# Summing x and beta of the last batch ahead in DRAM, earlier gathers and earlier weight loads in a fused attention and mixture-of-experts kernel

## The reference, cut to what matters

```
u   = ln_c(x)                                    # over the width, eps 1e-6
o   = conv1x1(channel_attention(u), wo)          # 8 heads of 16 channels, softmax over channels
x1  = x + (o - mean_w(o)) * rsqrt(var_w(o) + 1e-5) * gamma + beta       # over the width
t   = tokens(x1)                                 # 16 x 16384 x 128: rows of 128 numbers
z   = ln_t(t)
logits = z @ gate_w.T + gate_b ;  probs = softmax over the tokens of a batch
vals, idx = top 8 tokens of each of 64 experts, in each batch
pooled    = sum over the 8 of vals * z[idx]      # one row for each batch and expert
y   = gelu([pooled,1] @ weight1[e]) ; out_e = [y,1] @ weight2[e]
result = t ; result[idx] += vals * out_e
```

## Time and profile before

| | us |
|---|---|
| median of 3 runs (lowest, highest) | 2142.67 (2136.2, 2142.91) |
| the profiled execution | 2155.56 |
| its span, first to last instruction | 2153.8 |

### The profile page before, as it was taken

One profiled execution on the slowest core, in us unless ns is written; L12 is line 12 of the kernel. 1 busy time (PEld: TensorE's weight loads), 2 busy tenths in 40 slices (PEclk: granted clock), 3 DMA queues, 4 the chain that ended last, 5 costly groups with the idle time before them and its releaser, 6 DMA issues.

```text
span 2153.8 us, 42420 instructions
## 1 busy us (share of the span) xinstructions
PE 1873.0 (87%) x11917; PEld 1286.6 (60%) x11917; DVE 1822.8 (85%) x4612; ACT 1882.0 (87%) x5020; POOL 1939.2 (90%) x2068
## 2 busy tenths in 40 slices
PE   6999999999999999999999999999999987636991
PEld 6866666666666666666666666666666643213570
DVE  4689999999999898989899999999999899624670
ACT  6899999999999999999999999999999987743420
POOL 5799999999999999999999999999999999961387
PEclk9999999999999999999999999999999998765995
DMA  5498888887888888888788888888788676694963
GB/s 188 157 262 222 228 223 206 226 229 216 218 218 235 224 227 210 224 231 222 215 216 231 229 224 220 212 229 227 213 222 223 178 182 162 165 263 124 282 104 32
DMA packets 111068, 447.92 MB, mean 208 GB/s; under 512 B 10575, under 2 KB 52404, under 8 KB 61684
## 3 DMA queue, kind: packets, MB, share of 16 engines
q1 hardware_dynamic: 81140, 302.61, 42.9%
q0 software_dynamic: 29696, 142.61, 34.2%
HBM read 306.78 MB, written 138.41 MB: 207 GB/s over the span
## 4 chain that ended last, share of the span: by engine, by line
ACT 38%; POOL 21%; issue 17%; PE 16%; DVE 5%; ACTq 1%; DMA 1%; POOLq 0%; SPq 0%; DVEq 0%
ACT U L553 16%; POOL U L430 8%; POOL U L435 7%; ACT zT L516 6%; ACT UT L510 6%; PE G L747 4%; ACT LTS L580 3%; ACT LTS L525 3%; PE T L729 3%; PE O L680 2%; POOL zn L451 2%; POOL out_dram L490 2%; PE T L736 1%; ACT zn L574 1%; POOL U L442 1%
## 5 line engine op out<-in xcount | busy, mean ns | idle before, releaser
L553 ACT ACTIVATE U<-xa,nA,rA 128x128 f32<-128x128 f32 x1948 | 803.7, 483 | 2.1 <-issue 1.3
L747 PEld LDWEIGHTS G<-UT 128*128 128x128 f32 x4096 | 536.8, 192 | 226.5 <-issue 225.3
L430 POOL TENSOR_TENSOR U<-U,bet 128x512 f32<-128x512 f32 x512 | 651.4, 1272 | 2.2
L435 POOL TENSOR_TENSOR U<-U,rO 128x512 f32<-128x512 f32 x512 | 532.2, 1040 | 20.3 <-ACT rO L533 19.3
L747 PE MATMUL G<-UT 128*128 128x128 f32 x4096 | 542.0, 275 | 0.0
L680 PE MATMUL O<-U,MT 128*128 128x512 f32 x1024 | 529.5, 599 | 3.0 <-DVE U L938 3.0
L451 POOL TENSOR_TENSOR zn<-U,rZ 128x512 f32<-128x512 f32 x414 | 446.6, 1079 | 11.0 <-ACT rZ L564 10.3
L936 DVE BATCH_NORM_STATS2 stO<-O 128x6 f32<-128x256 f32 x1024 | 386.8, 423 | 50.2 <-PE O L680 49.5
L729 PE MATMUL T<-ident,U 128*128 128x128 f32 x2048 | 324.3, 281 | 119.1 <-ACT UT L510 108.6
L729 PEld LDWEIGHTS T<-ident,U 128*128 128x128 f32 x2048 | 224.6, 142 | 318.1 <-issue 314.1
L954 DVE BATCH_NORM_STATS2 stA<-xa 128x6 f32<-128x256 f32 x1024 | 386.8, 426 | 31.8 <-DMA xa<-in_x 28.5
(11 more groups left out here) (151 smaller groups left out, 1655.0 us busy)
## 6 DMA issues: line engine op xcount, KB each, us to landing
xa<-in_x SPq DMA_DIRECT2D x128, 1024.0 KB, 6.3
U<-in_x POOLq DMA_DIRECT2D x128, 1024.0 KB, 10.8
out_dram<-U SPq DMA_DIRECT2D x128, 1024.0 KB, 8.6
U<-in_L_ffn_weight SPq DMA_DIRECT2D x112, 256.0 KB
LTS<-in_L_ffn_weight SPq DMA_DIRECT2D x16, 256.0 KB
xa<-out_dram,UT POOLq DMA_INDIRECT x64
out_dram<-U,UT POOLq DMA_INDIRECT x64
zT<-in_L_ffn_weight SPq DMA_DIRECT2D x1, 128.0 KB
```

What stands on the lines that cost most here:

```text
L430: gp.tensor_tensor(rows(a, i), rows(a, i), bet_b, ALU.add).then_inc(S["gb"], 1)
L435: gp.tensor_tensor(rows(a, i), rows(a, i), rO[:, i // 2 % 2, i % 2 * TI:(i % 2 + 1) * TI].unsqueeze(2).to_broadcast([P, TI, W]), ALU.mult) ...
L553: last = sc.activation(utile(a, i, j), xa[:, k % XR, h * W:(h + 1) * W], ACT.Identity, scale=rA[:, k % 2, h:h + 1], bias=nA[:, k % 2, h:h ...
L747: last = te.matmul(G[:, 0:P], v, v, start=(i == 0 and j == 0), stop=(i == NI - 1 and j == TI - 1))
```

## The change

Three things are changed.

1. For the last batch (chunks 120 to 127, `X_BETA` = 120) POOL no longer adds beta. Instead x + beta is made ahead in DRAM, in the place of the result where the last batch will be stored. In step 100 SP writes beta, repeated over 16 image rows, from SBUF into the first 1 MB piece; in steps 116, 132, ..., 212 it copies that piece to the other seven. From step 260 on, one in 16 steps, POOL issues eight DMAs that add a piece of x (DRAM) to a piece of the result (DRAM). The accumulates of the last batch then read from there instead of from x.
2. `S_GATH` is 540, the gathers of 13 batches (52) stand three to two steps, and the first part of `PARTS` is at step 536 with 13 batches. The 12 other gathers stand behind the loop: four each for batches 13, 14 and 15. `Z_ALL` follows `S_GATH`, from 473 to 464, which moves items 467 and 471 of `zn` from POOL to ACT.
3. The weights of experts 0 to 15 stand in SP's body, one expert in two steps from step 540 on, each waiting only for the part of batch 14 that it overwrites. Experts 16 to 19 wait for items 0 to 7 of the last batch and the stores of its first two chunks, instead of the whole.

```diff
-PARTS = ((545, 0, 14), (576, 14, 15))
-S_GATH = 549
+PARTS = ((536, 0, 13), (577, 13, 15))
+S_GATH = 540
...
+X_BETA = 15 * NK
+S_PRE, S_SUM = 100, 260
...
         def _(sp): body
+                    if (m := ahead(b, t, S_PRE)) is not None:
+                        if m == 0:
+                            sp.dma_start(place(out_v, 0).rearrange("c b (h w) -> c (b h) w", w=W),
+                                         bet[:, :].unsqueeze(1).to_broadcast([P, TC, W])).then_inc(s_pre, 16)
+                        else:
+                            sp.wait_ge(s_pre, 16)
+                            sp.dma_start(place(out_v, m), place(out_v, 0)).then_inc(s_pre, 16)
...
+                    e, r = divmod(b[0] * NI + t - S_GATH, 2)
+                    if r == 0 and 0 <= e < EQN:
+                        wait_zn(sp, (NB - 2, None), e * 2 + 1)
+                        sp.wait_ge(s_store[e // 2], 16 * (NB // 2))
+                        weights(e)
...
-            wait_zn(sp, (NB - 2, None), NI - 1)
-            for k in range(NK):
-                sp.wait_ge(s_store[k], 16 * (NB // 2))
-            for e in range(EQN):
-                weights(e)
-            wait_zn(sp, (NB - 1, None), NI - 1)
-            for k in range(NK):
+            wait_zn(sp, (NB - 1, None), 2 * IC - 1)
+            for k in range(2):
                 sp.wait_ge(s_store[NK + k], 16 * (NB // 2))
...
         def _(pool): body
+                    if (m := ahead(b, t, S_SUM)) is not None:
+                        pool.wait_ge(s_pre, 16 * NX)
+                        gp.dma_start(place(out_v, m), place(x_v, m), accum_op=ALU.add).then_inc(s_sum, 16)
-                    if r := item(b, t, L_BETA):
+                    if (r := item(b, t, L_BETA)) and r[0][0] * NI + r[1] < X_BETA * IC:
...
-                                     x_v[:, bass.ds(bv, 1), k * CW:(k + 1) * CW],
+                                     (x_v if n < X_BETA else out_v)[:, bass.ds(bv, 1), k * CW:(k + 1) * CW],
...
-                    if 0 <= g < Q * (NB - 2):
+                    for g in range(max(0, 3 * g // 2), min(3 * (g + 1) // 2, Q * (NB - 3))):
```

More of the change, by code:

```diff
@@ L202, in program @@
         s_store = [sem(f"s_store{i}") for i in range(2 * NK)]
-        s_setup_dve = sem("s_setup_dve")
+        s_setup_dve = sem("s_setup_dve"); s_pre = sem("s_pre"); s_sum = sem("s_sum")
         names = ("a_bn a_ln a_rstd a_nmu u_ready tru ut_ready gram g_copied a1 a1s att att_s "
@@ L276, in wait_zn, with place, ahead @@
             wait(eng, S["zn_act"], by_act[n])
+        def place(v, m):
+            b, k = divmod(X_BETA + m, NK)
+            return v[:, b:b + 1, k * CW:(k + 1) * CW]
+        NX = NB * NK - X_BETA
+        def ahead(b, t, start):
+            m, r = divmod(b[0] * NI + t - start, 16)
+            return m if r == 0 and 0 <= m < NX else None
         def bodies(eng, body):
@@ L326, in body @@
                                      U[:, a[0] % 2, k:k + 1, :]).then_inc(s_store[n], 16)
-            bodies(sp, body)
+                    e, r = divmod(b[0] * NI + t - S_GATH, 2)
[3 more added lines that the diff above has]
+                        weights(e)
             def weights(e):
@@ L337, in weights @@
                              w2v[:, e:e + 1, :, :]).then_inc(landed, 16)
-            wait_zn(sp, (NB - 2, None), NI - 1)
-            for k in range(NK):
-                sp.wait_ge(s_store[k], 16 * (NB // 2))
-            for e in range(EQN):
-                weights(e)
-            wait_zn(sp, (NB - 1, None), NI - 1)
-            for k in range(NK):
+            bodies(sp, body)
+            wait_zn(sp, (NB - 1, None), 2 * IC - 1)
+            for k in range(2):
                 sp.wait_ge(s_store[NK + k], 16 * (NB // 2))
@@ L439, in body @@
                         a, k = r
-                        pool.wait_ge(S["gb"], cnt(a, NI, IC * k + IC))
+                        n = a[0] * NK + k
+                        if n < X_BETA:
+                            pool.wait_ge(S["gb"], cnt(a, NI, IC * k + IC))
+                        else:
+                            pool.wait_ge(S["y"], cnt(a, NI, IC * k + IC))
+                            pool.wait_ge(s_sum, 16 * NX)
                         bv = val(a)
                         gp.dma_start(U[:, a[0] % 2, k:k + 1, :],
-                                     x_v[:, bass.ds(bv, 1), k * CW:(k + 1) * CW],
+                                     (x_v if n < X_BETA else out_v)[:, bass.ds(bv, 1), k * CW:(k + 1) * CW],
                                      accum_op=ALU.add).then_inc(s_acc[a[0] % 2 * NK + k], 16)
@@ L460, in body @@
                                 pool.wait_ge(s_store[k], 16 * (NB // 2 - 1))
-                        gather(*divmod(g, NB - 2))
+                        gather(*divmod(g, NB - 3))
             bodies(pool, body)
[L467 to L473, removed]
+            for n in range(NB - 3, NB):
+                if n == NB - 1:
+                    pool.wait_ge(S["trz"], NB * NI)
+                    gp.memset(before, 1.0).then_inc(s_prep, 1)
+                    pool.wait_ge(s_prep, 2)
+                    gp.affine_select(out=before, in_=before, compare_op=ALU.is_gt, fill=0.0,
+                                     base=0, pattern=[[-1, P]], channel_multiplier=1).then_inc(s_prep, 1)
+                pool.wait_ge(R_["idx"], 3 if n == NB - 1 else 2)
                 for k in range(NK):
-                    pool.wait_ge(s_store[n % 2 * NK + k], 16 * (NB // 2))
+                    pool.wait_ge(s_store[n % 2 * NK + k], 16 * (n // 2 + 1))
                 for q in range(Q):
```

## The result

| | before, us | after, us |
|---|---|---|
| median of 13 runs each (lowest, highest) | 2139.51 (2135.4, 2142.91) | 2132.55 (2130.17, 2139.94) |
| the profiled execution | 2155.56 | 2130.77 |
| its span | 2153.8 | 2129.0 |

The ratio is 0.9972 [0.9961, 0.9983]: 7 us faster, where 21 were forecast. The interval leaves out 1, but the gain is no larger than the 0.3% or so that the prediction said can be told from no change. The direction and the range hold, the size does not.

A forecast was written before the change was run, and what follows sets the result against it. The prediction took ACT to bound the loop, with POOL close behind, and POOL the drain up to the last accumulate. A -11, B -14 and C +4 gave -21, carried to the median 2142.67 as 2121 us; range 2103 to 2143.

The forecast's parts named there:

- term B: ACT's two gaps behind the last accumulate, 18.2 us, blamed on the burst of weights; spreading it brings -14 us.
- rival 2: ACT's gaps behind the last accumulate stay: -11 + 4 = -7 us, 2136; chance 0.12.
- Term A: POOL up to the last accumulate: beta additions and zn items removed, 26 gathers added; -11 us.
- Term C: Copies and sums ahead in the steady loop: 0.25 us for each copy and sum, +4 us.
- The wait for `idx` (1.96 us) stays about as it is: POOL's first gather, two steps behind DVE's `places`, was to wait no longer when moved earlier.
- the far end: POOL's sum of -9.0 to -11.9 us, taken at -11 because early gathers fill idle time between steps 540 and 549.
- Rival 1: DMA engines become the bound from step 540 to 575, accumulates' cadence stays 15.0: -10 us, 2133; chance 0.14.
- Rival 3: Sums ahead delay accumulates and stall DVE in the loop: up to +45 us, together +20, 2163; chance 0.13.
- rival 4: All gaps gone, sums cost nothing, POOL's relief passed on in full: -30 us, 2113; chance 0.09.

The follow-up runs named there:

- after_again: The changed kernel unchanged, measured again on a third chip beside before: 2135.46 us, ratio 0.9897.
- b_again: The kernel before, unchanged, profiled and timed once more: 2138.01 against 2138.75 us, ratio 1.0.
- no_early_gathers: The changed kernel with gathers as before, one a step from step 549; beta ahead and weights spread stay: 2151.4 us, ratio 0.9973.
- no_early_again: The kernel of no_early_gathers once more, on the third chip: 2152.86 us, ratio 0.9982.
- no_spread: The changed kernel with the weights of experts 0 to 19 in one burst behind the loop, as before: 2134.08 us, ratio 0.9888.
- hold: The kernel before with all gathers from step 575 on held until PE has transposed the last item: 2165.2 us, ratio 1.0043.
- weights_again: The kernel of weights_alone once more, on a chip with gaps: 2159.44 us, ratio 1.0013.
- paced1: no_early_gathers with one gather a step from step 546, and from step 575 each waiting for PE's transposes: 2118.83 us, ratio 0.982.
- weights_alone: The kernel before with only the weights spread, experts 0 to 15 in SP's body from step 540: 2136.23 us, ratio 0.9991.
- beta_alone: The kernel before with only x + beta of the last batch summed ahead, gathers and weights as before: 2115.76 us, ratio 0.9888.
- from543: The changed kernel with gathers, three to two steps, from step 543 and the first part of the places at 539: 2127.76 us, ratio 0.9872.
- sum_unused: The kernel before plus the copies and sums in DRAM, their result unused and beta still added on POOL: 2156.4 us, ratio 1.0001.

## Why the prediction was right or wrong

**The difference carried over to the median: the step that failed.** The prediction took its sum against the profiled 2155.56 and then carried it to the median, "in which the same steps run". They do, but not with the same time: the 18.2 us of the earlier trace rows were in the profiled execution, and all 13 runs of the measurement are below 2143. Before's runs fall in two kinds: medians of 2139.51 and 2138.75 in the measurement and in the first group of experiments, 2158.01, 2156.53 and 2154.68 in the three others. Each of the four groups of experiments ran on a chip of its own, so "by the chip" is the likely reading, but no chip was taken twice. By its time and its gaps the profiled 2155.56 belongs with the slower kind; which chip it ran on is not known. The warning stood in the table: 12.9 us between a profile and its median, where a stall of 18.2 was about to be explained. Against a before with gaps the forecast of -21 is what after_again measured (-21); against the one of the measurement, without term B, it would have been -7, its rival 2, and that was measured.

Both agreements of the number are in part luck. The -7 of rival 2 is A's -11 and C's +4, and neither is right. Between the profiles of b_again and after, the last accumulate is 5.8 us earlier, the way from it to the last MAX8 1.7 us longer, and the experts' phase, from the gathers of the last batch to the end, 2.7 us shorter (199.8 and 197.1). That last part can't be put down to the change: the phase takes 197.1 us in after and 203.5 in after_again, the same kernel, and 203.9 and 196.8 in no_early_gathers and no_early_again. In the -21, A is some 4 us too much, B 3 too little and C 4 too much cost. In its sum the prediction also slipped in two places: 2142.67 - 21 rounds to 2122, and the terms' ranges give 2112 and not 2109 as the lower end. Neither decides anything.

**Term B, -14.** Its size against a before with gaps was a little low (17 of 18 us went). Its cause was wrong. Not the burst of weights holds ACT: no_spread and hold have the burst and no gap, weights_again and no_early_gathers gaps at a share of 0.20 and 0.19. What the gaps hang on is POOL's uninterrupted gathers behind the last accumulate: with them held the gaps go (hold), with most of them spaced they go too (paced1), and after, with eight of them ahead of those of the last batch, has none. They are not enough by themselves: b_again, weights_alone and beta_alone have as many on the chip without gaps. The Trainium skill ("Runtime: NRT & Kernel Launch", "Instruction fetch mechanics") says that crossing a block of instructions is mostly hidden, and rival 2 took from it that the burst would not hold ACT. The runs agree that it does not, but none shows whether fetches have a part in the gaps.

**Term A, -11.** Measured -5.8 between b_again and after (1884.9 to 1879.1), -6.9 against the profile shown. The count of instructions was right: the cadence is 12.5 us to the tenth, and over the last eight intervals 98.0 us instead of 112.9. What failed is "The wait for `idx` (1.96 us) stays about as it is" and the far end chosen because POOL idles there. The first gather waits 4.92 us instead of 1.96. Ahead of `places` DVE then has work of its own, of which two instructions take far longer than in before, 3.26 us instead of 0.85 and 2.40 instead of 0.39; why, no run shows. After, then before:

```profile
1749.51 3.26 DVE L1091 COPY UT<-ident 64x512 f32<-64x512 f32 x1
...
1761.32 2.40 DVE L1013 CAST tpf<-tp 128x8 f32<-128x8 uint32 x1
...
1768.11 0.19 DVE L958 CAST UT<-UT 128x52 uint32<-128x52 f32 x1
```
```profile
1759.07 0.39 DVE L979 CAST tpf<-tp 128x8 f32<-128x8 uint32 x1
...
1777.11 0.85 DVE L1057 COPY UT<-ident 64x512 f32<-64x512 f32 x1
```

The near end of the instructions, -9, and 3 us of wait are -6. With the gathers three steps later, from543 issues the last accumulate at 1874.7, after on the same chip at 1882.6; its first gather waits 2.24 us, and four gathers fewer, some 5 us, stand ahead of that accumulate.

**Term C, +4.** It is 0 (sum_unused 1.0001 [0.9989, 1.0013]). That a sum lands after 13.3 us and would put the next accumulate late did not come: after issues its accumulate 112, behind all eight sums, at 1685.7 where before has 1686.7. The latencies of 13.3 and 10.8 us did not add up: in all of after DVE waits 2.8 us for accumulates from x. The Trainium skill's formula ("DMA: Bandwidth & Descriptors", "Anatomy of one DMA — SWDGE (gpsimd) path") gave an estimate of 4.4 us. The sums take 13.3, so its figure does not hold here, and its term of 0 came out for another reason.

**Rival 1, the DMA engines.** Refuted: at a share of 1.04 and 282 GB/s the cadence is 12.5. The "about 270 to be had with accumulates in the mix" was too low. **Rival 3** is refuted by sum_unused. Of **rival 4** two conditions came true, no gap is left and C is nothing, and one did not: POOL's relief in full. Its 2113 was not reached.

**What the prediction did not ask.** It put the removed additions and the added gathers into one term and so did not see that removing beta is worth 23 us and the gathers moved ahead take back 17 of them (beta_alone against after; that the weights, which also differ, are worth nothing is weights_alone's). What they bring, fewer gathers behind the last accumulate, is only worth something where those make gaps: there, on the third chip, after is 17 us faster than it would be without them (2135.46 and 2152.86).

**Left open.** Why ACT starts so late on what PE has finished while gathers are issued, whether it is their issue on POOL or their transfers that matter, and why on some chips only. In the trace of before, PE's transposition that the first `zT` of the earlier trace rows needs ends at 1907.81, and ACT starts at 1920.87; what lay between them, the profile does not show.

```profile
1907.18 0.63 PE L736 MATMUL T<-ident,zn 128*128 128x128 f32 x4 [0.86 <-issue]
```

## What to carry to other kernels

Before a stall in a profile becomes a term, set the profiled execution beside the median of its runs: if they differ by about that stall, most runs may not have it, and a second profile of the same kernel tells. Sum a change part by part, each with its own sign; here the change without two of its parts (beta_alone) was 17 us faster than the whole. Gathers off the critical path belong where the engine that issues them has room. Behind the last critical transfer, spacing them by a wait for the engine that they would hold up was worth it here (paced1).

## What the runs showed of the hardware

- One program takes 2139 us on some chips and 2155 to 2158 on others. Between its two profiles, b_again and before, the spans differ by 18.0 us (2135.8 and 2153.8), and before has two waits of ACT for PE's products, 12.66 and 5.55 us, while GpSimd issues indirect DMAs 1.25 us apart. The same waits stand at a DMA share of 0.20 in weights_again (15.77 us) and of 0.19 in no_early_gathers (17.13 us).
- An add from DRAM to DRAM of 1 MB lands after 12.2 to 13.3 us and a copy after 12.5 to 14.2 (medians of each run), an accumulate from x into SBUF after 10.4 to 10.9; the last accumulate of hold after 8.0, at a DMA share of 0.77 (146 GB/s).
- Eight such adds and seven copies beside the loop cost nothing (1.0001 [0.9989, 1.0013]).
- The granted clock is 0.50, the lower level (1.2 GHz), in the second gap of no_early_gathers and in that of weights_again, where PE works 0.11 us of 10 and 0.00 of 14; from 1900 to 1910 in no_spread, where PE works 6.06 us, it is 0.83.
